# A graph network on one core: degrees and scales ahead of the first products, whose results become the table straight from PSUM

## The reference

```
h = relu(layernorm(x));  deg = segment_sum(1, dst incl. loops);  dinv = rsqrt(deg)
conv(h, W, b) = segment_sum((h @ W)[src] * dinv[src] * dinv[dst], dst) + b
x = x + conv(relu(conv(relu(conv(h, W1, b1)), W2, b2)), W3, b3)
h = relu(layernorm(x))
x = x + gru(segment_sum(h[src] + relvectors[rel], dst), h)
```

## Time and profile before

| | us |
|---|---|
| median of 3 runs (lowest, highest) | 969.9 (968.67, 970.46) |
| the profiled execution | 970.28 |
| its span, first to last instruction | 966.0 |
| PE busy | 914.8 (95%) |
| DVE busy | 478.7 (50%) |
| ACT busy | 288.2 (30%) |
| POOL busy | 51.5 (5%) |

### The profile page before, as it was taken

The page is one execution under the profiler, slowest core; times in us unless marked ns, Lnnn a source line. Parts: engine busy times, 40 slices in busy tenths (PEclk is TensorE's granted clock), DMA queues, the critical chain, the costliest instruction groups (busy, mean ns, idle before and its releaser), DMA issues.

```text
span 966.0 us, 16081 instructions
## 1 busy us (share of the span) xinstructions
PE 914.8 (95%) x6412; PEld 573.8 (59%) x6412; DVE 478.7 (50%) x1264; ACT 288.2 (30%) x567; POOL 51.5 (5%) x54
## 2 busy tenths in 40 slices
PE   2887899999999989999999999999999999999996
PEld 1665688888888875544445544444455455555553
DVE  7934898999999920101113143333525134333436
ACT  3354555555555521101111021112322021212222
POOL 0860010000000000000000000000000000000000
PEclk9998799999999999999999999999999999999999
DMA  7000000000000050000000011111131000100010
GB/s 209 5 1 1 1 13 14 18 13 13 13 13 13 12 159 1 2 1 0 1 1 1 28 44 32 34 44 44 60 105 36 8 22 22 33 23 22 22 33 30
DMA packets 27351, 27.67 MB, mean 29 GB/s; under 512 B 3217, under 2 KB 25901, under 8 KB 27272
## 3 DMA queue, kind: packets, MB, share of 16 engines
q1 hardware_dynamic: 26600, 26.18, 8.6%
q10 hardware_dynamic: 672, 0.41, 0.2%
HBM read 17.43 MB, written 9.15 MB: 28 GB/s over the span
## 4 chain that ended last, share of the span: by engine, by line
PE 90%; DVE 6%; ACT 2%; issue 1%; DMA 0%; SPq 0%; DVEq 0%; ACTq 0%
PE ps L1064 40%; PE ps L779 12%; PE ps L697 11%; PE ps L547 9%; PE ps L1075 4%; PE ps L551 4%; PE ps L757 3%; PE ps L1095 3%; DVE node_b L788 2%; PE ps L702 1%; PE ps L713 1%; PE ps L749 1%; PE ps L532 1%; PE ps L738 1%; ACT node_a L1013 0%
## 5 line engine op out<-in xcount | busy, mean ns | idle before, releaser
L1064 PE MATMUL ps<-count,node_b 128*128 128x512 f16 (+3 forms) x1400 | 271.2, 351 | 0.4 <-DVE node_b L1226 0.3
L788 DVE TENSOR_TENSOR node_b<-node_b 128x50 f16<-128x50 f16 (+4 forms) x455 | 209.6, 525 | 9.2 <-PE ps L697 8.9
L1064 PEld LDWEIGHTS ps<-count,node_b 128*128 128x128 f16 (+2 forms) x1400 | 121.5, 97 | 142.3 <-issue 8.2
L697 PE MATMUL ps<-node_b 128*128 128x225 f16 (+1 forms) x808 | 167.3, 291 | 16.2 <-DVE node_b L788 16.2
L989 ACT ACTIVATE count<-ps 128x500 f32 x202 | 122.8, 608 | 128.0 <-PE ps L697 121.7
L1064 PE MATMUL ps<-count,node_a 128*128 128x512 f16 (+3 forms) x700 | 135.4, 352 | 0.0
L779 PE MATMUL ps<-node_a,count 128*128 128x256 f16 (+1 forms) x924 | 131.7, 273 | 0.0
L1064 PEld LDWEIGHTS ps<-count,node_a 128*128 128x128 f16 (+1 forms) x700 | 59.9, 97 | 74.2 <-issue 7.2
L702 PE MATMUL ps<-node_b,params 128*128 128x9 f16 (+1 forms) x808 | 102.4, 175 | 0.0
L779 PEld LDWEIGHTS ps<-node_a,count 128*128 128x128 f16 (+1 forms) x924 | 88.8, 98 | 16.7 <-issue 4.3
L697 PEld LDWEIGHTS ps<-node_b 128*128 128x128 f16 x808 | 81.7, 102 | 25.0 <-DVE node_b L788 14.2
(11 more groups left out here) (205 smaller groups left out, 858.5 us busy)
## 6 DMA issues: line engine op xcount, KB each, us to landing
node_a<-in_x SPq DMA_DIRECT2D x4, 768.0 KB, 7.5
table_scratch<-agg SPq DMA_DIRECT2D x21, 128.0 KB, 1.7
node_b<-table_scratch SPq DMA_DIRECT2D x3, 768.0 KB, 6.7
xt<-x_scratch SPq DMA_DIRECT2D x16, 128.0 KB, 2.2
out<-scaled SPq DMA_DIRECT2D x16, 128.0 KB, 1.7
xt<-in_x SPq DMA_DIRECT2D x12, 128.0 KB, 2.0
params<-in_x SPq DMA_DIRECT2D x12, 128.0 KB, 2.0
x_scratch<-xt SPq DMA_DIRECT2D x12, 128.0 KB, 1.7
```

The lines of the kernel that those rows point to most:

```text
L697: return PE.matmul(window(s)[:, :, first:first + n], low, key_hot[k][j // 2][:, j % 2, :, i].rearrange("p (t w) -> p t w", w=n), start=(s ...
L788: return DVE.tensor_tensor(to, iota, keys.unsqueeze(2).to_broadcast([P, n, width, 2]), ALU.is_equal)
L1064: last = PE.matmul(ps[:, b, 0:cols], nodes[0:k, t, part, f * P:(f + 1) * P], count[0:k, t, c * CHUNK:c * CHUNK + cols], start=(n == 0 and ...
```

## The change

- Centring goes from POOL to ACT (an `activation` with the negated sum as bias, two beats ahead of the transposition). DVE's sum is negated for it.
- Ranks are counted with the one-hot row as the moving operand: 2 products of 404 columns to a beat, stationary a 20-column pick of the beat's row, into banks 5 and 7. ACT copies the 20 x 808 counts to SBUF, and 8 products with a 20-column identity turn them.
- The products with the first weights go from beats 11 to 35 to beats 40 to 64, behind the columns' sums, the scales and the degrees. They rotate over three banks. ACT reads the bank and writes the scaled high part, DVE reads the bank and writes the low part; the copy to SBUF (line 1013) is gone, and the bank is free when DVE has read.
- The table needs no shifted tiles. The 1050 products of the first convolution begin at step 18 and are spread evenly over 184 steps, target tile by target tile.

```diff
-        WEIGH_AT = TURN_AT + 3
+        CENTRE_AT = 6
+        COUNTS_AT = 24
+        COLUMNS_AT = 25
-        COLUMNS_AT = WEIGH_AT + T + 1
-        WEIGHT_AT = 34
-        DEGREE_AT = 46
-        SCALE_AT = 49
-        FACTORS_AT = 58
+        WEIGHT_AT = 28
+        SCALE_AT = 33
+        DEGREE_AT = 36
+        WEIGH_AT = 40
+        FACTORS_AT = 42
-        LOW_PART_AT = FACTORS_AT + 10
+        LOW_PART_AT = WEIGH_AT + 8
+        PRODUCTS_FROM = (WEIGH_AT + T) // BEATS + 2
+        early_products = [(u, t, part) for u in range(EARLY) for t in range(T) for part in range(2)]
...
             if beat < WINDOW:
                 PE.wait_ge(ranks_ready, beat + 2)
+                for h, bank in enumerate(counts_bank):
+                    last = PE.matmul(ps[0:WINDOW, bank, 0:EACH // 2], picks[:, WINDOW - 1 - beat:2 * WINDOW - 1 - beat],
+                                     rank_is[beat][:, h * EACH // 2:(h + 1) * EACH // 2], start=(beat == 0), stop=(beat == WINDOW - 1))
...
             if 0 <= t < T:
-                PE.wait_ge(x_turned_out, t + 1)
-                PE.wait_ge(*((x_weighted_out, t) if t else (w_early_in[0], 16)))
+                if t == 0:
+                    PE.wait_ge(w_early_in[0], 16)
+                    PE.wait_ge(x_turned_out, T)
+                    PE.wait_ge(root_due.sem, 2)
+                    PE.wait_ge(columns_read, 1)
+                elif t >= 3:
+                    PE.wait_ge(table_ready, t - 2)
                 for f in range(HALVES):
-                    last = PE.matmul(WEIGHED[0:m, :], turned_x(t)[:, f, 0:m], w_early[0][:, f, :], ...)
+                    last = PE.matmul(weighed(t)[0:m, :], turned_x(t)[:, f, 0:m], w_early[0][:, f, :], ...)
...
-                DVE.scalar_tensor_tensor(out=table0(t)[0:m, 1, :], in0=h1[0:m, t, :], ...)
+                DVE.scalar_tensor_tensor(out=node_a[0:m, t, 1, :], in0=weighed(t)[0:m, :], ...)
...
+            t = beat - CENTRE_AT
+            if 0 <= t < T:
+                ACTE.wait_ge(x_summed, min(t // 6, XG) + 1)
+                ACTE.activation(h1[0:m, t, :], h1[0:m, t, :], ACT.Identity, bias=moments[0:m, t, 0:1], scale=2.0).then_inc(x_centred, 1)
...
-                ACTE.activation(h1[0:m, t, :], WEIGHED[0:m, :], ACT.Copy).then_inc(x_weighted_out, 1)
-                ACTE.activation(table0(t)[0:m, 0, :], h1[0:m, t, :], ACT.Copy, scale=newt[0:m, 0, t:t + 1]).then_inc(table_high, 1)
+                ACTE.activation(node_a[0:m, t, 0, :], weighed(t)[0:m, :], ACT.Copy, scale=newt[0:m, 0, t:t + 1]).then_inc(table_high, 1)
```

More of the change, by code:

```diff
@@ L148, in program @@
         EACH = QUARTERS * NS
+        assert EACH % 2 == 0 and EACH // 2 <= BANK
         assert ASIDE > ASIDES and ASIDE + 2 * EACH <= CW and at[0] <= 6 * CW and WINDOW == 20 and T == 25
@@ L441, in x_sums_dve @@
             DVE.wait_ge(x_stats, end)
-            DVE.tensor_tensor(moments[:, first:end, 0], x_raw[:, first:end, 1], x_raw[:, first:end, 4], ALU.add).then_inc(x_summed, 1)
+            DVE.scalar_tensor_tensor(out=moments[:, first:end, 0], in0=x_raw[:, first:end, 1], scalar=-1.0, in1=x_raw[:, first:end, 4],
+                                     op0=ALU.mult, op1=ALU.subtract).then_inc(x_summed, 1)
         def x_variance_dve():
@@ L636, in program @@
[L636 to L645, removed]
@@ L647, in program @@
+        assert products_after[-1] == len(early_products)
         assert all(settled(u) < s for s, n in enumerate(products_after) for u, _, _ in early_products[:n])
-        summed_at = [next(s for s in range(NS) if (u, T - 1, 1) in early_products[:products_after[s]]) for u in range(EARLY)]
-        def table0(t):
-            return [n[:, :].bitcast(F16).rearrange("p (a d) -> p a d", a=2) for n in (*scaled, xt[0])][t] if t < SHIFT else node_a[:, t - SHIFT, :, :]
+        summed_at = [next(s for s in range(NS) if products_after[s] >= (u + 1) * 2 * T) for u in range(EARLY)]
@@ L774, in early_product_pe @@
                     PE.wait_ge(conv_read, u - OUT_SLOTS + 1)
[L775 to L779, removed]
+                else:
+                    PE.wait_ge(table_ready, T)
+            last = PE.matmul(out_slot(u)[0:m, :], count[0:k, t, u * P:u * P + m], node_a[0:k, t, part, :],
                              start=(t == 0 and part == 0), stop=(t == T - 1 and part == 1), skip_group_check=True)
@@ L881, in beside_dve @@
                 DVE.wait_ge(*dve_seq.now)
-                DVE.wait_ge(counts_done, WINDOW)
-                DVE.tensor_tensor(high_of, high_of, CNT.rearrange("p (w i) -> p w i", i=2).unsqueeze(2).to_broadcast([P, WINDOW * Q // 2, T, 2]),
-                                  ALU.mult).then_inc(hist_due, 1)
+                DVE.wait_ge(counts_done, 1)
+                for q in range(Q):
+                    some = high_of[0:lanes(q), q * WINDOW // 2:(q + 1) * WINDOW // 2, :, :]
+                    cnt = CNT[0:lanes(q), q * WINDOW:(q + 1) * WINDOW].rearrange("p (w i) -> p w i", i=2)
+                    DVE.tensor_tensor(some, some, cnt.unsqueeze(2).to_broadcast([lanes(q), WINDOW // 2, T, 2]), ALU.mult).then_inc(hist_due, 1)
             if beat == DEGREE_AT:
@@ L921, in scale_dve @@
                 DVE.wait_ge(abs_summed, 1)
-                DVE.tensor_reduce(fours[:, 0:2], COLUMNS, AX_X, ALU.max).then_inc(*dve_seq.up())
+                DVE.tensor_reduce(fours[:, 0:2], COLUMNS, AX_X, ALU.max).then_inc(columns_read, 1)
             elif step == 1:
                 DVE.wait_ge(small_reduced, 1)
-                DVE.wait_ge(*dve_seq.now)
+                DVE.wait_ge(columns_read, 1)
                 DVE.scalar_tensor_tensor(out=bounds[:, 0:1], in0=fours[:, 0:1], scalar=TOP, in1=fours[:, 2:3],
@@ L1008, in beside_act @@
                 ACTE.activation(turned_x(t)[:, :, 0:m], TURNED[:, :, 0:m], ACT.Relu).then_inc(x_turned_out, 1)
+            if beat == WINDOW - 2:
+                ACTE.wait_ge(ranks_counted, 1)
+                for h, bank in enumerate(counts_bank):
+                    ACTE.activation(counts_t[0:WINDOW, h * EACH // 2:(h + 1) * EACH // 2], ps[0:WINDOW, bank, 0:EACH // 2],
+                                    ACT.Copy).then_inc(counts_out, 1)
+            if beat == VARIANCE_AT - AHEAD_ACT:
+                x_root_act()
+            if beat == DEGREE_AT - AHEAD_ACT:
+                inverse_root_act(degree[:, 3, :], [degree[:, i, :] for i in range(3)])
             t = beat - WEIGH_AT
```

61 lines of the change are left out of this document (29 added, 32 removed).

## The result

The changed kernel takes 964.35 us (median of 5 runs, 963.56 to 965.95) against 969.98 for the kernel before on the same chip: ratio 0.9943, 95% interval 0.9929 to 0.9958. It is 5.6 us faster; the forecast was 968.6, 1.3 faster, in a range of 961.0 to 974.5. The profiled execution took 963.61, its span 959.3, 6.7 less than before.

What follows compares the result with a forecast made beforehand. PE's own work was taken to set the pace from 108 us on. Step 18 at 103.8 against 105.4 for break-even gave 1.6 us, 1.3 after an allowance: 970.3 - 1.3 = 969.0, less 0.4 is 968.6, range 961 to 974.5.

Steps and rivals of the forecast that it cites:

- The sum's own case: Whole kernel: the terms hold as summed, 966 to 971.5 us, given half the chance.
- the rival of the high clock: Transpositions and after: PE's clock stays high, 6.3 us more gain, 962.3 us; chance 0.22.
- From step 18 to the mark: First convolution's products to the last copy's end (issue row): PE's own work sets the pace, 238.2 us.
- Up to the first transposition: Kernel's start, with two windows and the counts of beats 4 to 7: transposition starts at 35.0 us.
- Ring: Repeating PE-ACT cycle of the transpositions: 0.99 us a beat at the full clock, 1.23 at the low.
- The clock held up by the wide counts: Beats 8 to 19: wide counts keep PE streaming at the full clock, 12.9 us.
- Degrees at 68.2: Degrees end at 68.2 us, with beats 20 to 31 at the low clock (15.3) and the degrees taking 1.6.
- Weights' products 0.91 a tile: Products with the first weights, ahead of step 18: 25 tiles at 0.91, 22.8 us.
- Stalls behind DVE's pairs: Weights' products: PE waits for DVE's pairs, 0.4 us twice and 1.7 at the end.
- Low clock at the weights' start: First tiles of the weights' products run at the low clock, costing 1.3 us more.
- Low parts from PSUM cost no more: DVE's low parts: 0.476 us from PSUM, 0.477 from SBUF; the skill's rule would cost some 1.6 us more.
- ScalarE sets the ring: Transpositions: ACT's centring doesn't fit, each of 24 beats costs 0.09 to 0.1 more, +2.3 us, 970.9; chance 0.10.

Runs made afterwards that it cites:

- after: The changed kernel itself, without further edits, against the kernel before: 964.35 us, ratio 0.9943.
- e10: Changed kernel with the first convolution's 1050 products begun at step 28 instead of 18: 970.25 us, ratio 1.0000 to the kernel before.
- e7: Changed kernel with the last self loops ahead of the last output tile's two DVE instructions: 962.71 us, ratio 0.9923 to the kernel before.
- e9: Changed kernel with the sums of the weights' columns at beat 20 instead of 25: 965.12 us, ratio 0.9948 to the kernel before.
- e2: Changed kernel with ranks counted as before, eight single-column products a beat, no copies or turning: 966.01 us, ratio 0.9963 to the kernel before.
- e4: Changed kernel with idle 384-column PE products added behind transpositions of beats 20-24 and 28-31 and behind step 9: 963.19 us, ratio 0.9927 to the kernel before.
- e12: Changed kernel with centring on GpSimd in the old form, multiply and subtract with the plain sum: 969.73 us, ratio 1.0001 to the kernel before.
- e1: Changed kernel with centring back on GpSimd as multiply and add with the negated sum: 962.57 us, ratio 0.9932 to the kernel before.

## Why the prediction was right, step by step

The direction was right, and the time lies in the range, but the size was not: 1.3 us were forecast and 5.6 measured. The sum's own case, 966 to 971.5, doesn't hold 964.35; it lies between that case and the rival of the high clock, 962.3. Two terms were too dear, and one condition of the gain was not understood.

- *From step 18 to the mark*, 238.2: measured 238.3 in after. This largest term, PE's own work by its rows, held to a tenth, and e10 shows the condition under which it holds: products beside the windows from the start, or DVE makes the pace.
- *Up to the first transposition*, 35.0: 35.13, by luck. The sum left out beat 8's two products (0.64 here), and the first window ran at the full clock, 0.75 instead of 1.08; in e7, e10 and e9 the same place is at 34.7, 36.3 and 36.6. *Ring* 0.99 at the full clock: 0.97, and 1.22 at the low one in e9. *The clock held up by the wide counts*: yes, by e2.
- *Degrees at 68.2*: they ended at 65.57 (64.40 + 1.17), 2.6 early. The step that failed is that beats 20 to 31 all run at the low clock (15.3, with sums and turning 17.8). From the first of them to the degrees it took 15.4: the clock stayed up until 52.0, though the last wide counts end at 47.3, and it rose again at 58.8, with the column sums (e9). I had priced these sums by their length alone. The degrees took 1.17 for 1.6.
- *Weights' products 0.91 a tile*: 0.86, so 25 x 0.05 = 1.25 early. I divided the whole piece of 3.65 us by four tiles; a piece contains the last product's tail. The starts of that same row's products are 0.215 apart, 0.86 a tile. I knew it for the wide counts and didn't do it here.
- *Stalls behind DVE's pairs* 0.4 twice and 1.7 at the end: 0.28, 0.32 and 1.47. *Low clock at the weights' start* 1.3: the first four tiles took 4.32, 0.9 too long. 103.8 - 2.6 - 1.25 = 99.95, where step 18 is, and the smaller terms cancel; since e7 and e10 start it at 101.1, inside the 101 to 106 of the forecast, one of these 3.8 is that execution's luck.
- *Low parts from PSUM cost no more*: 0.48 with the bank as source, as the earlier trace rows had it. The Trainium skill's dearer start from PSUM (VectorE: DVE Perf Modes, the TRN2 errata) isn't seen here. The Trainium skill's rule that matmuls which stay back to back keep the clock and waits between them lose it (TensorE: Matmul & The Clock Gate, Loop structure matters more than you think) agrees with e2 (transposition pair 0.66 against 0.41), e4 (1.00 against 0.76 from 48 to 76) and e9 (0.50 at 62 to 64).
- *The rival of the high clock*, 962.3, was half true: the clock was high until 52.0 and from 58.8 to 65.7, low between and behind. *ScalarE sets the ring* was nearer than its 0.10: it has 0.19 to spare in a plain beat, but in the four beats of step 6, with two copies of counts in its queue, these take 4.9 us and with GpSimd centring 4.1.
- *Not seen at all*: that centring stood ahead of the maximum over partitions in GpSimd's queue. The sum took ScalarE's centring as a way to feed the ring and gave it price 0; without it, or GpSimd's faster form, the change would have gained nothing (e12). The direction came out right because the part was there, not because it was understood. That is luck.
- *Two small readings*: DVE's 478.7 is 52% of PE's 914.8, not half or less, and 0.38 + 0.61 + 0.4 is 1.39, not 1.35. Nothing hangs on either.

The gain is therefore: step 18's products 4.2 to 5.4 us earlier than break-even (105.4 against 101.2 and 100.0), and in the one profile another 1.4 behind the mark, where the dip is missing. The medians are 5.6 apart; how much of that is the dip's isn't shown.

## What to carry to other kernels

When a result is moved ahead, look up every queue that it passes, the slow engine's too: what stood harmlessly behind 36 us of other work may become the path. Take the price of a repeated instruction from the distance of starts, never from a piece's length. And ask of long unbroken work on PE what it does to the clock of what follows, not only how long it takes: here the wide counts kept the clock up, and it rose with the column sums.

## What the runs showed of the hardware

- GpSimd's `tensor_scalar` on 128x256 f32: multiply and add 0.53 us, multiply and subtract 1.15 (medians of 25 in the same stretch, e1 and e12; the programs differ besides only in DVE's sums for it). The means are 0.77 and 1.46, as the early ones take longer in both.
- Between the last centring and the maximum over partitions GpSimd stood 5.59 us (e12), 5.58 (e1) and 5.76 (before) with nothing to wait for in the profile. What it does there no run tells.
- The granted clock read 1.00 from 32 to 58 in e2 (and from 30 to 42 before) while a pair of transpositions took 0.66, the low rate. Durations are the safer witness early in a trace.
- Behind the pause of 2.4 us at the mark the clock dips in six of eleven profiles and not in the other five, 1.7 us each time. With the microsecond by which step 18 differs between programs alike up to there (after, e7, e10), the span of a single profile of this kernel decides little below 2 us.
